# One-hot compares of a graph kernel: four windows side by side become four rows of columns

## The reference

```python
edge_index = jnp.stack([src, dst])
x = _layernorm(x + _L0_gnn_ref(x, edge_index, ...))   # three rounds: segment_sum(h[src], dst), linear, batch norm, relu
x = _layernorm(x + _L1_gnn_ref(x, edge_index, ...))   # mean over neighbours, two linears
x = _layernorm(x + _L2_gnn_ref(x, edge_index, ...))   # mean, two linears, batch norm
x = _layernorm(x + _L3_gnn_ref(x, edge_attr_128, src, dst, edge_weight, ...))   # weighted max, then weighted mean
```

## Time and profile before

| what | us |
|---|---|
| median of 3 runs | 4930.73 |
| lowest and highest | 4900.83, 4937.73 |
| the profiled execution's own time | 4922.53 |
| its span (first to last instruction) | 4920.7 |
| first compare begins | 60.59 |
| VectorE begins the last two compares | 937.43 |

### The profile page before, as it was taken

How to read it: one execution, slowest core, us unless ns; L and a number is a source line. 1 busy time by engine, 2 the same in 40 slices (tenths; PEclk the granted TensorE clock), 3 DMA queues, 4 the chain that set the end, 5 groups by cost and what they waited for, 6 DMA issues and landing times.

```text
span 4920.7 us, 57973 instructions
## 1 busy us (share of the span) xinstructions
PE 3483.8 (71%) x22119; PEld 2928.1 (60%) x22119; DVE 2147.8 (44%) x4433; ACT 1956.0 (40%) x3073; POOL 1782.5 (36%) x1727
## 2 busy tenths in 40 slices
PE   4899999921112997995118999983477686877678
PEld 2677777611002996994108989973355565665566
DVE  7776676610001986884012233242233333333335
ACT  4677777710000444554005546552222222222221
POOL 3000000077773000777760000005555555556530
PEclk9999999955555998997559989996788898889889
DMA  4878788800002667442004424423255555556555
GB/s 146 228 213 230 214 219 231 240 21 7 7 7 47 223 236 236 151 130 53 4 7 140 133 72 144 130 62 108 71 196 185 193 189 191 188 197 214 170 183 179
DMA packets 299723, 712.84 MB, mean 145 GB/s; under 512 B 65270, under 2 KB 167445, under 8 KB 284214
## 3 DMA queue, kind: packets, MB, share of 16 engines
q1 hardware_dynamic: 167180, 436.77, 27.7%
q10 hardware_dynamic: 52298, 174.64, 9.9%
q0 software_dynamic: 79968, 97.68, 9.2%
HBM read 503.59 MB, written 254.50 MB: 154 GB/s over the span
## 4 chain that ended last, share of the span: by engine, by line
PE 53%; another core or an unknown queue 25%; DVE 7%; issue 6%; ACT 6%; DMA 2%; ACTq 1%; DVEq 0%; SPq 0%
PE PS L740 21%; PE PS L1725 7%; PE PS L662 6%; PE PS L625 5%; PE PS L1711 3%; PE PS L671 2%; PE PS L1701 2%; DMA turned<-DEG 2%; PE PS L1693 2%; DVE BB L1877 2%; ACT DEG L884 1%; PE PS L718 1%; ACT CA L859 1%; DVE PAN L549 1%
## 5 line engine op out<-in xcount | busy, mean ns | idle before, releaser
L431 POOL DMA_INDIRECT PAN<-table,src_i x832 | 826.6, 994 | 1359.1 <-DMA table<-DEG 769.7
L972 POOL DMA_INDIRECT shares<-dst_f,spare x832 | 886.7, 1066 | 738.1 <-ACTq L777 426.8
L740 PE MATMUL PS<-CX,XH 125*128 125x376 f32 x2000 | 477.8, 318 | 261.6 <-issue 181.2
L740 PE MATMUL PS<-CX,XL 125*128 125x376 f32 x2000 | 472.9, 315 | 141.9 <-issue 141.9
L740 PEld LDWEIGHTS PS<-CX,XH 125*128 125x128 f32 x2000 | 321.3, 197 | 279.9 <-issue 219.9
L1819 ACT ACTIVATE BB<-PS 128x1024 f32<-128x1024 f32 x104 | 106.5, 1024 | 938.5 <-PE PS L1701 567.6
L625 PE MATMUL PS<-hot 128*128 128x250 bf16 x1250 | 382.7, 397 | 34.7 <-ACT CA L859 20.3
L537 ACT ACTIVATE CX<-PAN 125x3125 fp32r<-125x3125 uint8 x106 | 298.2, 2815 | 271.1 <-PE PS L740 233.6
L740 PEld LDWEIGHTS PS<-CX,XL 125*128 125x128 f32 x2000 | 321.7, 197 | 141.5 <-issue 141.5
L740 PE MATMUL PS<-CP,XH 125*128 125x376 f32 (+1 forms) x1330 | 310.7, 313 | 120.3 <-DVE XL L1070 63.0
L1701 PE MATMUL PS<-ident,BB 128*128 128x128 f32 x832 | 141.5, 325 | 310.6 <-DVE BB L1877 249.6
(11 more groups left out here) (334 smaller groups left out, 6998.0 us busy)
## 6 DMA issues: line engine op xcount, KB each, us to landing
PAN<-counts SPq DMA_DIRECT2D x300, 390.6 KB
shares<-SSB ACTq DMA_DIRECT2D x70, 1600.0 KB
XP<-shares SPq DMA_DIRECT2D x50, 1600.0 KB
PAN<-shares SPq DMA_DIRECT2D x50, 1600.0 KB
BB<-start_penalty SPq DMA_DIRECT2D x104, 512.0 KB
shares<-blank ACTq DMA_DIRECT2D x15, 3200.0 KB, 13.7
turned<-DEG SPq DMA_DIRECT2D x50, 781.2 KB, 9.3
PAN<-turned SPq DMA_DIRECT2D x100, 390.6 KB
```

The lines of the kernel that those rows point to most:

```text
L431: nc.gpsimd.indirect_dma_start(out=gbuf[g % 2][:, k, :], out_offset=None, in_=source, in_offset=bass.IndirectOffsetOnAxis(ap=src_i[:, t:t ...
L740: last = nc.tensor.matmul(wide_ps[b][h][:, 0:w], halves[part][0:TN, s * SUBJ + j, :], cast_part(v, j, h), start=(s == 0 and j == 0 and par ...
L972: nc.gpsimd.indirect_dma_start(out=shares_flat, out_offset=bass.IndirectOffsetOnAxis(ap=share_at[:, t:t + 1], axis=0), in_=share[:, t:t + ...
```

## The change

The one-hots of four windows no longer alternate element by element. Each window has its own run of columns: `hot_lo` is now 4 rows of 128, `hot_key` 8 rows of 125 (two halves for each of four windows). `iota_h` is the plain row of 128 numbers, read again for each window (outer step 0). The key of a window is repeated along its columns: in the second operand the innermost dimension has a step of 0. The number of instructions, of elements and of semaphore operations stays. The matmuls read weights and columns with a step of one element.

```diff
--- before.py
+++ after.py
@@ -131,8 +131,8 @@
         ST = [sb(f"ST{b}", [128, TPB, D]) for b in range(2)]
         hot_size = QUAD * (128 + 2 * TN)
         hot = nc.alloc_sbuf_tensor_at("hot", [128, RING * hot_size], BF16, offset=at_hot)
-        hot_lo = [hot[:, r * hot_size:r * hot_size + QUAD * 128].rearrange("p (n w) -> p n w", w=QUAD) for r in range(RING)]
-        hot_key = [hot[:, r * hot_size + QUAD * 128:(r + 1) * hot_size].rearrange("p (a n w) -> p a n w", a=2, w=QUAD)
+        hot_lo = [hot[:, r * hot_size:r * hot_size + QUAD * 128].rearrange("p (w n) -> p w n", w=QUAD) for r in range(RING)]
+        hot_key = [hot[:, r * hot_size + QUAD * 128:(r + 1) * hot_size].rearrange("p (w n) -> p w n", w=2 * QUAD)
                    for r in range(RING)]
         src_i = sb("src_i", [128, T + 2 * GT], I32)
         dst_f = sb("dst_f", [128, T])
@@ -219,7 +219,7 @@
         pairs_of = [BB[:, 1664:2176], AA[:, 3072:4096], AA[:, 4096:5120]]
         win_of = [BB[:, 2176:2176 + 5 * 128], AA[:, 5120:5120 + 5 * 256]]
         win_junk = [BB[:, 4064 + j * T // 2:4064 + (j + 1) * T // 2].bitcast(BF16) for j in range(4)]
-        iota_h = firsts[:, 0:128 * QUAD].rearrange("p (n w) -> p n w", w=QUAD)
+        iota_h = firsts[:, 0:128]
         slot_lo = src_i[:, :].bitcast(BF16)
         near_w, near_k, same, before, behind = (BB[0:G, j * KRW:(j + 1) * KRW] for j in range(5))
         near_i = near_k.bitcast(I32)
@@ -621,8 +621,9 @@
                 if n > 1:
                     pe.wait_ge(pair_kept, n - 1)
                 for x in range(count):
-                    keys = hot_key[u % RING][:, i % 2, :, :].rearrange("p n (w a) -> p w a n", w=2)[:, x, :, :]
-                    last = nc.tensor.matmul(pair_ps[n % 2][:, x, :], hot_lo[u % RING][:, :, 2 * (i % 2) + x], keys,
+                    at = 2 * (i % 2) + x
+                    keys = hot_key[u % RING][:, 2 * at:2 * at + 2, :].rearrange("p a n -> p (a n)")
+                    last = nc.tensor.matmul(pair_ps[n % 2][:, x, :], hot_lo[u % RING][:, at, :], keys,
                                             start=True, stop=True)
                 last.then_inc(pair_made, 1)
 
@@ -1147,7 +1148,7 @@
         def dve_build(dve):
 
             placed_after(dve, nc.vector.tensor_copy(ident_h[:, :], ident[:, :]))
-            placed_after(dve, nc.vector.tensor_copy(iota_h, iota[:, :].unsqueeze(2).to_broadcast([128, 128, QUAD])))
+            placed_after(dve, nc.vector.tensor_copy(iota_h, iota[:, :]))
             nc.vector.memset(ident_r[:, 0:1].bitcast(F32), 0.0)
             nc.vector.memset(ident_r[:, TN + 1:128].bitcast(F32), 0.0)
             placed_after(dve, nc.vector.tensor_copy(ident_r[0:TN, 1:TN + 1], ident[0:TN, 0:TN]))
@@ -1161,13 +1162,13 @@
                 if u >= RING:
                     dve.wait_ge(pair_made, quad_pairs(u - RING))
                 r = u % RING
-                nc.vector.tensor_tensor(out=hot_lo[r], in0=iota_h,
-                                        in1=slot_lo[:, w:w + QUAD].unsqueeze(1).to_broadcast([128, 128, QUAD]),
+                nc.vector.tensor_tensor(out=hot_lo[r], in0=iota_h.unsqueeze(1).to_broadcast([128, QUAD, 128]),
+                                        in1=slot_lo[:, w:w + QUAD].unsqueeze(2).to_broadcast([128, QUAD, 128]),
                                         op=ALU.is_equal)
-                keys = slot_key[:, 2 * w:2 * w + 2 * QUAD].rearrange("p (a w) -> p a w", a=2)
+                keys = slot_key[:, 2 * w:2 * w + 2 * QUAD]
                 nc.vector.tensor_tensor(out=hot_key[r],
-                                        in0=iota_h[:, 0:TN, :].unsqueeze(1).to_broadcast([128, 2, TN, QUAD]),
-                                        in1=keys.unsqueeze(2).to_broadcast([128, 2, TN, QUAD]),
+                                        in0=iota_h[:, 0:TN].unsqueeze(1).to_broadcast([128, 2 * QUAD, TN]),
+                                        in1=keys.unsqueeze(2).to_broadcast([128, 2 * QUAD, TN]),
                                         op=ALU.is_equal).then_inc(hot_full, 1)
 
             shares_made = 0
```

## The result

Before, 20 executions have a median of 4925.59 us; after, 20 have 4945.45 us. The ratio is 1.0041 with a 95% interval of 1.0024 to 1.0058: about 20 us more, small but clear of noise. The forecast was 4924 us, no change, in a range of 4885 to 4983.

What follows compares the result with a forecast made beforehand. TensorE was taken to set the pace from 367 us on, VectorE after the change. Stretches summed to -5.5 us, refound waits added +6.5: +1 us on 4922.5, so 4924 us, range 4885 to 4983.

Steps and rivals of the forecast that it cites:

- both prices: VectorE's compares at one element at a time: 1.20 us large, 0.685 small; +0.80 or +0.65 us a quad.
- second rival: Contiguous columns don't speed the matmul, 128 rows of edges or the output cause its 0.22 us: 4963 us, chance 0.09.
- VectorE as the bound: Compare stage: TensorE's gain is spent on VectorE, which becomes the bound of the stage; total +1 us.
- refound waits: Late stretches: TensorE and VectorE close in odd ones, some waiting comes back, 0.5 us for each of 13, +6.5.
- key waits: Stretches 2 to 5: VectorE waits until TensorE reaches the transposed keys, some 3 us or less each; now 24.4 in five.
- sum for stretches 7 to 18: 192 quads, half at each price: 364.93 + 96 x 0.80 + 96 x 0.65 = 504.1 against 530.06 us, -26.0.
- no DMA is added: Whole kernel: only the copy of the row of numbers shrinks, worth at most 0.3 us; nothing else is moved.
- fast rival: Compares stay at two elements at a time, TensorE keeps the bound: 4801 us, or 4841 if DMA takes a third; chance 0.12.
- signs named in advance: Compares 1.20 and 0.68 us, matmul starts 0.11 apart, VectorE's wait some 10, TensorE's 50 to 65, full clock, stretches 7 to 18 500 to 515.
- low end of the range: Whole program without refound waits and with shorter key waits: 4905 us, less the scatter of runs 4885.
- stretch 2: VectorE's 47.57 us + 19 quads x 0.65 + 4 for gaps and key waits = 63.9 us, +6.6.
- third rival: Two compare buffers stop hiding the hand-over, 0.43 us a quad on 205 quads of stretches 7 to 19: 5012 us, chance 0.09.

Runs made afterwards that it cites:

- with the writes moved: The changed kernel with ACT's writes of blank regions issued behind other steps, same bytes: 3777.56 us, ratio 0.9967 to the kernel before.

## Why the prediction was wrong

**Right: both prices.** The large compare was put at 1.20 us and measures 1.191; the small one at 0.685, and it measures 0.686 in the changed kernel. A repeated 2-byte element took the operation to one element at a time, in the second source (1191 ns) and in the first (1193 ns). The Trainium skill reports this in the section named in the prediction ("Vector Engine (DVE) Microarchitecture Reference", 5.1); the traces agree, for either source. The matmuls start 0.11 us apart:

```profile
431.05 0.38 PE L626 MATMUL PS<-hot 128*128 128x250 bf16 x2
431.27 0.48 PE L663 MATMUL PS<-CA,HH 125*128 125x375 bf16 x2
```

Two take 0.22 us where two took 0.44. Only the layout differs, so the step of 8 bytes was the cause and the second rival is out. Weights and columns lost this step together, and no run separates the two. The rule that the Trainium skill gives in "Advanced Engine Details and Errata", section SBUF Cachelines, by which two hits on a line are enough, does not hold for these matmuls; the measurement decides.

**Right: VectorE as the bound, where nothing else is.** In us, with the refound waits of 0.5 a stretch counted in:

| stretches | before | predicted | measured |
|---|---|---|---|
| 0 | 26.9 | 33.1 | 32.5 |
| 1 | 47.4 | 41.9 | 42.2 |
| 2 | 57.3 | 63.9 | 69.1 |
| 3 to 6 | 174.8 | 191.2 | 184.0 |
| 7 to 18 | 530.1 | 510.1 | 531.0 |
| 19 | 41.5 | 38.7 | 41.7 |
| sum | 877.9 | 878.9 | 900.6 |

Of the 7 us by which stretches 3 to 6 were put too high, 3.3 are the key waits (9 us were allowed, VectorE idled 5.7) and 3.9 are VectorE's busy time.

**Wrong: the late stretches.** The step that failed is the sum for stretches 7 to 18, "504.1 against 530.06", with "VectorE is the bound", and beside it "no DMA is added". I compared two engines, TensorE and VectorE, and took the longer; the wait of ACT for the staged writes had no term. The third party was in the rows: a DMA share of 0.87 in stretch 7. I used it for the fast rival alone. By my sum the odd stretches come to 39.5 us, and the DMA work of stretch 7 (0.87 x 43.90 = 38 us) would nearly fill them. A mean share tells too little even so: in steps of 5 us it is 1.04 to 1.13 from 395 to 410 us and 0.10 from 420 to 425. The kernel before had the same crowding (1.12 from 375 to 385 us), and ACT's 11.5 us of waits for staged writes were a sign of it. What the runs showed in place of VectorE's bound: ACT waits 32.7 us for staged writes in stretches 7 to 18, TensorE 27.5 us for ACT's copies behind them, and it goes away with the writes moved. Of 20.9 us missed there, all is in the odd stretches: five of the six measure 43.7 to 45.0 us. Stretch 19, which is of the same kind, has 3.0 us more. With the writes moved, stretches 7 to 18 take 494.4 us, 10 us less than even the bare sum of 504.1; VectorE's work is 487.5 and had been put 17 too high.

So the size of the miss is partly luck: VectorE's busy time, too high by 16 us in the late stretches and 4 before, hid a good part of what the staged writes cost. Most of these 16 us can be told from the rows, by an estimate: before, nearly each quad ended in a wait (166 in stretches 7 to 18), and the last 0.08 us of its last instruction (375.36 to 375.44 us in the trace, say) counted as busy; after, the next compare starts within them. 166 x 0.08 = 13 us.

Of the signs named in advance, the prices and the starts of L626 came true. VectorE's wait for TensorE fell to 53.7 us and not to some 10 (15.0 with the writes moved). TensorE waited 40.2 us for the compares in stretches 7 to 18, where 50 to 65 had been named for the late ones, and these stretches took 531 us and not 500 to 515. The clock did not stay at full speed: it is 0.98 in stretches 7 to 18. The low end of the range is also worked out wrongly, but by little: without refound waits (6.5 us) and with the shortest key waits (9 us) 4924 becomes 4908.5 and not 4905.

**Wrong: stretch 2, by 5 us.** Once slice 0 is written from its buffer, ACT may fill it again. Before, this wait was 3.1 us; now TensorE comes to it earlier, and it is 8.9. From ACT's timeline:

```profile
146.40 1.16 ACT L860 ACTIVATE CA<-PS 128x500 bf16<-128x500 f32 x2 [8.92 <-DMA counts<-CA]
```

VectorE then waits 4.12 us for a free buffer. VectorE's busy time in this stretch was put right (59.9 us), so the 5 us are all idle time. It is the same kind of error, a write that the old pace had covered. That these 5 us come from it was read from the trace and not tried by itself. The granted clock of the stretch fell as well, from 0.94 to 0.80; what that costs was not separated.

**The third rival** (the hand-over of the two buffers in each quad) is out: with the writes moved VectorE waits 15.0 us in 11 waits in the whole stage, and none in stretch 7.

## What to carry to other kernels

A gain on the bounding engine is only as large as the distance to the next bound, and that is to be read in each stretch for every queue and buffer, DMA in steps of a few microseconds too, not as a mean share. When a stage gets shorter, look at which transfers now fall into less time, and at which buffer's write-out was covered by the old pace; moving writes of the same bytes gave 40 us of the stage here, and nothing in the kernel before. And an operand that is repeated need not cost the paired mode: a key written twice side by side, read with an innermost step of 1 and count of 2, kept it (0.676 us for 1008 elements).

## What the runs showed that was not expected

- The rest of the program has two levels. In one set of runs the medians of all kernels lie between 3750 and 3830 us, in the others between 4810 and 4950. The changed kernel was profiled at both levels: from 1050 to 1550 us TensorE is busy 436 us at the faster level and 74 at the slower. The kernel before, at the slower level, has gaps of over 60 us in its chain between 1053 and 1537 us while GpSimd issues its scatters; TensorE then starts one instruction each 2.8 us with no wait that the profile shows:

```profile
1062.78 0.37 PE L740 MATMUL PS<-CX,XL 125*128 125x250 f32 x1 [2.33 <-issue]
1065.58 0.47 PE L740 MATMUL PS<-CX,XH 125*128 125x376 f32 x1 [2.43 <-issue]
```

At the faster level TensorE starts matmuls of the same kind 0.26 us apart at 1050 us, at a granted clock of 0.51, and 0.14 us apart from 1052 us on, at the full clock, with the scatters going on. The slower level keeps a clock of 0.50 from 1050 to 1550 us. Which level a set gets, and why, stays open; the kernel before and the changed kernel were both seen at either.

- The small compare reads keys in runs of four. It took 0.42 us where a run starts on an even element and 0.56 on an odd one; with the repeated key it is 0.686 us in both, and with doubled keys 0.425.
- Weight loads of the compares went from a median of 113 to 99 ns with contiguous weights. No run separates what that is worth from the faster columns.
